# The shared-expert stage of a two-layer transformer block: weights loaded during the last batch, its rows kept in SBUF, the router and the tables of tiles reordered

## The reference

```python
scores = sigmoid(gate_w @ x) + gate_b            # 16 experts
weights, indices = top_k(scores, 4); weights /= weights.sum()
shared_out = (silu(x @ w1_shared) * (x @ w3_shared)) @ w2_shared
h3 = silu((x @ w1_routed[e]) * (x @ w3_routed[e]))
return shared_out + sum_over_chosen_e(weight_e * (h3 @ w2_routed[e]))
```

## Time and profile before

| | |
|---|---|
| time, median of 3 runs | 1366.03 us (1360.82 to 1368.21) |
| the profiled execution | 1364.2 us, its span 1362.4 us |
| busy in the span | PE 1257.5 us (92%), DVE 847.7 us (62%), ACT 596.2 us (44%), POOL 472.7 us (35%) |
| granted PE clock, mean | 0.975 of full speed |
| DMA | 112.20 MB, mean 82 GB/s |

### The profile page before, as it was taken

The page is one execution under the profiler, slowest core; times in us unless marked ns, Lnnn a source line. Parts: engine busy times, 40 slices in busy tenths (PEclk is TensorE's granted clock), DMA queues, the critical chain, the costliest instruction groups (busy, mean ns, idle before and its releaser), DMA issues.

```text
span 1362.4 us, 25374 instructions
## 1 busy us (share of the span) xinstructions
PE 1257.5 (92%) x9326; PEld 1095.7 (80%) x9326; DVE 847.7 (62%) x1733; ACT 596.2 (44%) x1351; POOL 472.7 (35%) x488
## 2 busy tenths in 40 slices
PE   5699989999988879999988899999999999999996
PEld 4588878778777757777767888899999999998995
DVE  4647567557556654434447777776666767676785
ACT  3333323323323335555544444445454545555552
POOL 0112332332431220000028787644434344434442
PEclk9799999989999989999999999999999999999998
DMA  5754224234100953333331221100000000000000
GB/s 203 280 194 152 104 103 151 78 129 148 47 33 27 346 188 105 105 103 103 109 121 53 67 65 47 63 1 32 1 1 32 1 32 1 1 1 1 1 32 32
DMA packets 63674, 112.20 MB, mean 82 GB/s; under 512 B 6977, under 2 KB 36033, under 8 KB 62017
## 3 DMA queue, kind: packets, MB, share of 16 engines
q1 hardware_dynamic: 57408, 93.79, 19.6%
q0 software_dynamic: 6144, 16.79, 3.7%
HBM read 49.86 MB, written 60.69 MB: 81 GB/s over the span
## 4 chain that ended last, share of the span: by engine, by line
PE 82%; DVE 8%; issue 4%; ACT 3%; another core or an unknown queue 2%; DMA 1%; POOL 0%; SPq 0%; ACTq 0%; DVEq 0%; POOLq 0%
PE bank L703 7%; PE six L720 6%; PE six L817 5%; PE bank L779 4%; PE bank L781 4%; PE bank L780 4%; PE bank L390 4%; PE bank L391 3%; PE bank L392 3%; PE bank L854 2%; PE bank L853 2%; PE bank L852 2%; PE bank L791 2%; PE six L831 2%; PE bank L792 2%
## 5 line engine op out<-in xcount | busy, mean ns | idle before, releaser
L1799 POOL TENSOR_TENSOR rstd<-msq,half_pow 128x8 f32<-128x8 f32 x64 | 105.4, 1647 | 156.6 <-DVE msq L1610 156.2
L1128 ACT ACTIVATE pT<-six,rstd 128x256 f32<-128x256 f32 x128 | 60.7, 475 | 215.3 <-PE six L818 212.9
L1736 POOL TENSOR_TENSOR hid_l<-hid,hid_h 128x256 fp32r<-128x256 f32 x64 | 48.0, 750 | 241.2 <-ACT hid_h L950 241.2
L1811 POOL TENSOR_TENSOR pT<-pT,tri_mul 128x512 f32<-128x512 f32 x64 | 84.3, 1316 | 129.1 <-ACT pT L1174 129.1
L1212 DVE TENSOR_TENSOR yT1l<-six,yT1h 128x512 fp32r<-128x512 f32 x64 | 44.3, 692 | 135.5 <-ACT yT1h L1179 135.5
L1603 DVE TENSOR_TENSOR sq<-xs 128x512 f32<-128x512 f32 x128 | 104.2, 814 | 17.2 <-ACT xs L1147 17.2
L703 PE MATMUL bank<-experts,xT 128*128 x316 | 109.5, 469 | 0.8 <-ACT xT L1072 0.8
L779 PE MATMUL bank<-bw_h,xT1h 128*128 128x512 f32 x256 | 106.2, 415 | 0.7 <-issue 0.7
L781 PE MATMUL bank<-bw_l,xT1h 128*128 128x512 f32 x256 | 100.5, 392 | 0.0
L780 PE MATMUL bank<-bw_h,xT1l 128*128 128x512 f32 x256 | 100.1, 391 | 0.0
L817 PE MATMUL six<-qT,kT 128*128 128x256 f32 x256 | 79.3, 392 | 19.0 <-issue 15.6
(11 more groups left out here) (282 smaller groups left out, 3926.7 us busy)
## 6 DMA issues: line engine op xcount, KB each, us to landing
cells_scratch<-zeros SPq DMA_DIRECT2D x8, 4352.0 KB, 14.8
xg<-cells_scratch SPq DMA_DIRECT2D x79, 128.0 KB, 2.0
cells_scratch<-y SPq DMA_DIRECT2D x79, 128.0 KB, 1.7
experts<-pack_experts_dram SPq DMA_DIRECT2D x16, 608.0 KB
raw<-pack_attn_dram SPq DMA_DIRECT2D x8, 1024.0 KB
raw<-pack_w_dram SPq DMA_DIRECT2D x2, 1024.0 KB
xT_scratch<-xT1h_c SPq DMA_DIRECT2D x8, 256.0 KB, 2.1
xT_scratch<-xT1l_c SPq DMA_DIRECT2D x8, 256.0 KB, 2.7
```

Of the source, the lines that this page charges most:

```text
L1799: pool.tensor_tensor(out=rstd[:, r, :], in0=msq[:, r, :], in1=half_pow[:], op=ALU.pow).then_inc(rstd_sb, 1)
```

## The change

- **Loads.** During batch 7 SP already issues the `xT1h` loads of sequences 0 to 5, once the last keys are made (`xT1h` lies where layer 0's query and key weights were), and experts 0 to 5 and `xT1h` of sequence 6 once the last scores are transposed; the `xT1l` loads and experts 6 to 10 follow when the last up projections and the last mix of values are made, and experts 11 to 15 where the loads used to begin. The SBUF layout is reordered so that dead tensors lie under these loads (`w2_h`, `w2_l`, `yt0` and what is used longest move to the end).
- **Sequence 7's transposed norm** is written straight to its place in `xT1h`/`xT1l` (`own_h`, `own_l`, by a `norm_T1_last` on ACT and DVE). Its store and loads and the wait between them are gone.
- **Order at the end of batch 7.** DVE does `out_T` and `gate_out` behind router part 1 of sequence 6 and ahead of parts 2 to 4, which used to come before them; ACT does `out_T` ahead of `gate_out`.
- **Router.** Its steps are split anew. For sequence 7, DVE normalises at m = 2 and makes part 0 at m = 5, each ahead of the tile's own steps, ranks and selection (1, 2) at m = 6, slots (6) at m = 7 and weights (5) at m = 8. PE makes transposes and logits ahead of the tile's `shared_up` at m = 3 and 4 and the positions at m = 7; ACT follows.
- **Tables.** Each partition works out one tile: the steps are 16 columns wide instead of 1280 (`own_tile` is a column 0 to 127 that comes as a constant). Two small matmuls (`tables_T`, m = 12) turn the two columns into a row, the second one packing four experts into a number, and one DVE copy (`tables_row`) hands it on. The steps start at m = 9 instead of 11.
- SP reads the registers of the first eight cells before its wait for the sends instead of behind it.

```diff
@@ -313,27 +320,41 @@
-            def load_norm(b):
-                sp.wait_ge(xT1_stored, 32 * (b + 1) if b == NB - 1 else 32 * (NB - 1))
-                for s, part in enumerate((xT1h, xT1l)):
-                    sp.dma_start(part[:, :, b * T:(b + 1) * T].bitcast(F32),
-                                 xT1_dram[s, b].rearrange("p (k t) -> p k t", k=KD)).then_inc(xT1_loaded[b], 16)
+            def load_norm(b, s):
+                sp.dma_start((xT1h, xT1l)[s][:, :, b * T:(b + 1) * T].bitcast(F32),
+                             xT1_dram[s, b].rearrange("p (k t) -> p k t", k=KD)).then_inc(xT1_loaded[b], 16)
...
-            for b in range(NB - 1):
+            last = NB - 1
+            for b in range(last - 1):
...
+            sp.wait_ge(k0_ps, 2 * NB)
+            sp.wait_ge(xT1_stored, 32 * (last - 1))
+            for b in range(last - 1):
+                load_norm(b, 0)
+            store_norm(last - 1)
+            sp.wait_ge(sT0_ps, NG * NB)
+            sp.wait_ge(cells_cleared, 16 * NB)
+            for e in range(6):
+                load_expert(e)
+            sp.wait_ge(xT1_stored, 32 * last)
+            load_norm(last - 1, 0)
+            sp.wait_ge(y0_ps, NG * NB)
+            sp.wait_ge(up_ps, NJ * NB)
+            for b in range(last):
+                load_norm(b, 1)
+            for e in range(6, 11):
+                load_expert(e)
             sp.wait_ge(yT0_ps, NB)
-            for b in range(NB - 1):
-                load_norm(b)
-            for e in range(10):
-                load_expert(e)
-            store_norm(NB - 1)
-            load_norm(NB - 1)
-            for e in range(10, NE):
+            for e in range(11, NE):
...
@@ -355,8 +376,8 @@
             sp.wait_ge(tables_made, 1)
+            c = cells(0, GROUP)
             sp.wait_ge(cells_sent, 16 * TT * TOPK * NB)
-            c = cells(0, GROUP)
...
@@ -512,6 +533,13 @@
+            def tables_T(bank):
+                pe.wait_ge(tile_cols, 2)
+                n = NG1 * GROUP
+                pe.matmul(bank[0:1, 0:n], t_cols[:, 0:1], ident[:, 0:n], start=True, stop=True)
+                pe.matmul(bank[0:1, n:n + n // PACK], t_cols[:, 1:2], pack_by_4, start=True, stop=True).then_inc(tile_rows, 1)
...
@@ -724,15 +752,17 @@
                     pe.wait_ge(slot_sb, NB)
-                shared_up(m)
...
                 if m == 4:
-                    logits_T(t, six[:, 1, :])
-                if m == 5:
+                    logits_T(t, six[:, 1, :], (own_h, own_l))
+                shared_up(m)
+                if m == 4:
                     logits(t, six[:, 0, :])
-                if m == 9:
+                if m == 7:
                     positions(t, six[:, 1, :], True)
+                if m == 12:
+                    tables_T(six[:, 0, :])
...
@@ -1346,18 +1384,19 @@
                 if part == 2:
+                    link(dve.tensor_tensor(out=r_sel[:], in0=r_rank[:].unsqueeze(2).to_broadcast(kths),
+                                           in1=kth.unsqueeze(1).unsqueeze(3).to_broadcast(kths), op=ALU.is_equal))
+                if part in (3, 5):
...
                                            op=ALU.mult))
-                    link(dve.tensor_tensor(out=r_sel[:], in0=r_rank[:].unsqueeze(2).to_broadcast(kths),
-                                           in1=kth.unsqueeze(1).unsqueeze(3).to_broadcast(kths), op=ALU.is_equal))
...
                     link(dve.tensor_reduce(out=prob_all[:, bass.ds(TT * b, TT), :], in_=r_tmp[:], axis=AX.X, op=ALU.add))
-                if part == 3:
+                if part in (4, 6):
...
@@ -1458,11 +1497,16 @@
                     router(t, 1)
+                if final:
+                    out_T(b)
+                    gate_out(b)
+                if not first:
                     router(t, 2)
+                    router(t, 3)
...
                 if not first:
-                    router(t, 3)
+                    router(t, 4)
...
@@ -1516,23 +1558,19 @@
                 link(dve.tensor_tensor(out=t_end[:], in0=t_first[:], in1=t_count[:], op=ALU.add))
-                link(dve.tensor_tensor(out=t_ge[:], in0=tile_index.unsqueeze(2).to_broadcast(wide),
-                                       in1=t_end[:].unsqueeze(1).to_broadcast(wide), op=ALU.is_ge))
+                link(dve.tensor_tensor(out=t_ge[:], in0=own_tile.to_broadcast([P, NE]), in1=t_end[:], op=ALU.is_ge))
                 link(dve.tensor_reduce(out=t_expert[:], in_=t_ge[:], axis=AX.X, op=ALU.add))
-                link(dve.tensor_tensor(out=t_base[:], in0=t_ge[:], in1=t_count[:].unsqueeze(1).to_broadcast(wide),
-                                       op=ALU.mult))
+                link(dve.tensor_tensor(out=t_base[:], in0=t_ge[:], in1=t_count[:], op=ALU.mult))
                 link(dve.tensor_reduce(out=t_before[:], in_=t_base[:], axis=AX.X, op=ALU.add))
-                link(dve.tensor_tensor(out=t_before[:], in0=tile_index, in1=t_before[:], op=ALU.subtract))
-                link(dve.scalar_tensor_tensor(out=t_before[:], in0=t_expert[:], scalar=float(NT), in1=t_before[:],
-                                              op0=ALU.mult, op1=ALU.add))
-                link(dve.tensor_scalar(out=t_expert[:], in0=t_expert[:], scalar1=float(NE - 1), scalar2=None, op0=ALU.min))
-                dve.tensor_copy(tile_cell[:], t_before[:])
-                four = t_expert[:].rearrange("p (n k) -> p n k", k=PACK)
-                for k in (2, 1):
-                    link(dve.scalar_tensor_tensor(out=four[:, :, k], in0=four[:, :, k + 1], scalar=float(NE),
-                                                  in1=four[:, :, k], op0=ALU.mult, op1=ALU.add))
-                dve.scalar_tensor_tensor(out=tile_pack[:], in0=four[:, :, 1], scalar=float(NE), in1=four[:, :, 0],
-                                         op0=ALU.mult, op1=ALU.add).then_inc(tables_made, 1)
+                link(dve.tensor_tensor(out=t_before[:], in0=own_tile, in1=t_before[:], op=ALU.subtract))
+                dve.scalar_tensor_tensor(out=t_cols[:, 0:1], in0=t_expert[:], scalar=float(NT), in1=t_before[:],
+                                         op0=ALU.mult, op1=ALU.add).then_inc(tile_cols, 1)
+                dve.tensor_scalar(out=t_cols[:, 1:2], in0=t_expert[:], scalar1=float(NE - 1), scalar2=None, op0=ALU.min)\
+                   .then_inc(tile_cols, 1)
+            def tables_row(bank):
+                dve.wait_ge(tile_rows, 1)
+                dve.tensor_copy(tile_row[0:1, :], bank[0:1, 0:NG1 * GROUP + NG1 * GROUP // PACK]).then_inc(tables_made, 1)
...
@@ -1566,26 +1604,29 @@
             for m in range(NS):
+                if m == 2:
+                    normalise(t, xn1_last, mv1, rs1, rs1_sb, xn1_sb)
+                if m == 3:
+                    norm_T1_last(t, six[:, 0, :])
+                if m == 5:
+                    router(t, 0)
...
                     stats(t, st1, mv1, ve1, st1_sb, mv1_sb, ve1_sb, NB)
-                if m == 2:
-                    normalise(t, xn1_last, mv1, rs1, rs1_sb, xn1_sb)
-                if m == 3:
-                    norm_T1(t, six[:, 0, :])
                 if m == 6:
-                    router(t, 0)
+                    router(t, 1)
+                    router(t, 2)
                 if m == 7:
-                    router(t, 1)
+                    router(t, 6, six[:, 1, :], True)
                 if m == 8:
-                    router(t, 2)
+                    router(t, 5)
                 if m == 9:
-                    router(t, 3, six[:, 1, :], True)
-                if m == 11:
                     tables()
+                if m == 12:
+                    tables_row(six[:, 0, :])
...
```

More of the change, by code:

```diff
@@ L148, in build @@
         g1 = sc("g1", [P, NT, D])
+        own_h, own_l = (part[:, :, (NB - 1) * T:NB * T] for part in (xT1h, xT1l))
         sc = region(XT_END, LATE)
@@ L225, in build @@
             "kT1_sb", "rden1_sb", "y1_sb", "yT1l_sb", "acc1", "bw_lo", "v1_ones"))
[L227 to L228 removed]
+        sh_hi, sh_lo, table, tile_cols, tile_rows, tables_made, experts_loaded = (sem(n) for n in (
+            "sh_hi", "sh_lo", "table", "tile_cols", "tile_rows", "tables_made", "experts_loaded"))
         xg_loaded = [sem(f"xg_loaded{j}") for j in range(GROUP)]
@@ L493, in logits_T @@
                 for k in range(KD):
-                    last = three(bank[:, 0:T], gate[0][:, k, :], gate[1][:, k, :], xT1h_c[:, k, :], xT1l_c[:, k, :],
+                    last = three(bank[:, 0:T], gate[0][:, k, :], gate[1][:, k, :], xT1[0][:, k, :], xT1[1][:, k, :],
                                  k == 0, k == KD - 1)
@@ L678, in shared_up @@
                 after(pe, u2_sb, m - 1)
-                if m % TT == 0:
+                if m % TT == 0 and m // TT < NB - 1:
                     pe.wait_ge(xT1_loaded[m // TT], 32)
@@ L961, in norm_T1, with norm_T1_last @@
                 act.activation(xT1h_c[:].rearrange("p k t -> p (k t)"), bank, ACT.Copy).then_inc(xT1h_sb, 1)
+            def norm_T1_last(b, bank):
```

(18 more changed lines are left out.)

33 lines of the change are left out of this document (15 added, 18 removed).

## The result

The kernel with the change takes 1358.9 us (median of 20 runs, 1356.2 to 1363.4). Beside it on the same chip the kernel before took 1364.0 us (20 runs, 1360.4 to 1369.6). The ratio is 0.9963, with a 95% interval of 0.9952 to 0.9974: 5.1 us. That is clear of the noise, but under the 0.5% at which the prediction puts its line. 1359.2 was forecast. The profiled execution took 1357.2 us, 7.0 less than that of before.

What follows compares the result with a forecast made beforehand. PE, busy 92% of the span, was taken as the bound, with 18.1 us excess in the shared-expert stage. Terms 0 + 0.7 - 0.9 - 7.8 + 0.4 + 1.7 = -5.9 us gave 1359.2 us, range 1354 to 1364.5.

Steps and rivals of the forecast that it cites:

- The tables (-7.8): Shared stage: DVE's tables block shrinks from 9.7 to 3.6 us, PE's stall from 9.7 to 1.9; gain 7.8 us.
- The row of tables: Two small PE matmuls and one DVE copy at m = 12 cost 0.4 us, bounds 0.2 and 1.5.
- The sends of sequence 7 (+1.7): Shared stage: 5 to 10 us after sends begin, PE's results reach others late; costs 1.7 us, bounds 0 and 3.9.
- The end of batch 7 (+0.7): Reordered end of batch 7: first up product 0.3 us later, first tiles at half clock 0.4; bounds 0 and 1.7.
- The router (-0.9): Sequence 7's norm and router moved earlier in the shared stage gain 0.9 us; bounds a loss of 1.0, gain of 2.8.
- m = 7 starts about 1.5 us later than before: Part of the router term: the earlier norm and router delay shared tile m = 7 by about 1.5 us.
- With a stall of 1.7 us already paid: Part of the router term: by m = 7 a stall of 1.7 us is already paid, giving net 0.9 us.
- still fall on it: POOL's first sends, starting at 451.04 whatever is changed, still fall on router part 0, now at m = 5.
- Neither the expert weights nor sequence 7's norm set the start: Routed stage's start: PE's last tiles, made late by DVE, set it; SP issues row loads 4.6 us ahead.
- the sends are hidden: Rival, 0.27: sequence 7's sends cost nothing and the logits tile loses its whole excess; -9.5 us, about 1355.5.
- One wait for another: Rival, 0.25: sends' stall, router part 0, half clock and slower first tiles add up; -1.7 us, about 1364.
- The loads hurt batch 7: Rival, 0.06: weight loads from 429 on delay instruction fetches at batch 7's end; +9.7 us, about 1375.

Runs made afterwards that it cites:

- f1: The changed kernel unchanged, on a chip without late answers, beside the kernel before (1336.6 us): 1328.7 us, ratio 0.994.
- e6: The kernel before with the new tables, their row at m = 14, and sequence 7's norm kept in SBUF: 1364.6 us, ratio 0.999.
- e3: The changed kernel without the sends of sequence 7, so its output lacks rows, on a chip without late answers: 1328.6 us (one run).
- e4: The changed kernel without any sends of rows or the waits for them, on a chip without late answers: 1329.5 us, ratio 0.9942 to the kernel before.
- f3: The changed kernel without any sends again, on a chip without late answers: 1330.0 us, ratio 0.9949 to the kernel before.
- second pair: Profiles of the kernel before and the changed kernel, both unchanged, on a chip with late answers: 1368.0 us (one run) and 1362.5 us.
- e1: The kernel before with the new tables alone, at m = 11, their row at m = 14: 1337.3 us, ratio 1.0005.
- r_before: The kernel before, unchanged, run for its profile on a chip with late answers: 1368.0 us (one run).
- r_after: The changed kernel, unchanged, on a chip with late answers: 1362.5 us, ratio 0.9978 to the kernel before.
- f2: The changed kernel with all norm and weight loads issued at the old place, on a chip without late answers: 1329.1 us, ratio 0.9942 to the kernel before.
- e5: The kernel before with sequence 7's norm kept in SBUF alone, no store, wait or reload: 1365.9 us, ratio 1.0004.

## Why the prediction was right in its total, and where it was not

**The tables (-7.8) were right**, with the rest of the change in place. The block is 3.3 us (3.6 forecast). Tile m = 11 takes 4.02 us, 1.97 over the undisturbed 2.05 (1.9 forecast); before, the tables' tile and the next lost 9.24 + 0.46 = 9.7. The clock stayed full. **The row of tables** cost 2.52 - 2.05 = 0.47 us at m = 12 in f1, where nothing else disturbs that tile (+0.4).

**The sends of sequence 7 (+1.7)** came out in size: from m = 11 on the changed kernel takes 15.17 us where answers are late and 13.36 in f1 where they aren't, 1.8 us, most of it in tile m = 12 (4.10 against 2.52), in the expected place, 10 us behind the first send. In e6 the sends start 9.4 us later (479.91), and the wait of DVE for "remote" comes with them: it ends at 489.25, 9.3 us behind the first send, and in the changed kernel at 480.43, 10.0 behind. So the lateness follows the sends in time. But the row of tables moved along with them, to m = 14, and no run takes the sends away where answers are late, so the cause is not shown. Without late answers the sends cost nothing (e3, e4, f3), and both kernels without sends ran where none are late. It stays open whether sends alone bring them on; batch 1, which sends nothing and waits 3.3 us, still speaks for it.

**The end of batch 7 (+0.7)** was +0.35 in this pair. The 0.3 was right. The half clock did come: m = 0 to 2 ran at a mean granted clock of 0.73 of full speed (partly 1.2, partly 2.4 GHz), against 0.82 before, and PE was busy for all 6.27 us instead of 5.65; it cost nothing here because the old order had 0.6 us of waits in these tiles. In the second pair the two rows of the table are +0.86 and -0.06. In e1 and f1, the old and the new order where no answers are late, they are +0.37 and +1.23 (clock 0.96 and 0.75 in m = 0 to 2): up to 1.6 us, near the upper bound.

**The router (-0.9) is the step that failed: the gain isn't there.** m = 3 to 10 take +0.98 us in this pair (24.03 to 25.01) and -0.10 in r_before and r_after (26.51 to 26.41). Only where no answers are late is it -1.0 (21.39 us in e1, with the old order, and 20.35 in f1). The working had two parts. "m = 7 starts about 1.5 us later than before" was +2.3 us from the last `out_T` in this pair, +1.6 in the second and +1.5 between e1 and f1: right but for the first. "With a stall of 1.7 us already paid" was to give that back and more. It gave back 1.0, 0.9 and 1.0, since a stall came in that the prediction has at nothing: `positions`, moved up to m = 7, stands one tile behind the steps that feed it, and PE waits 0.81 us for `r_cum` (0.82 in f1, f2 and f3). Together with the end of batch 7, the way from the last `out_T` to m = 11 was forecast 0.2 us shorter and is 1.3, 0.7 and 0.6 us longer.

What made the first part worse in this pair is the late answers of sequence 6's sends, which "still fall on it". Over e1 and f1 they cost 24.03 - 21.39 = 2.6 us in the old order and 25.01 - 20.35 = 4.7 in the new one. Of the 4.7, m = 4 and 5 have 0.9 and 3.6 (3.10 and 5.63 us against 2.18 and 2.05); m = 6, with router part 0, takes 3.96 against 3.78, so its own stall is paid in full behind the late answer, as it was three tiles later in the old order. In the second pair the same sums are 5.1 and 6.1 us, part of it a half clock in both (0.94 and 0.87 over m = 3 to 10). The sums set traces of different chips against each other, so they price the late answers and don't explain them.

**"Neither the expert weights nor sequence 7's norm set the start" was true of the kernel before, and wrong as a price.** The early loads are worth nothing where no answers are late (f1 against f2, 0.03 us in the stretch). The norm in SBUF is also worth nothing alone (e5), but without it and the earlier router the tables' term is nothing too (e1: 6.62 us of wait for `xg`). I read 4.6 us between SP's issue and PE's transpose as slack of the chain. It was time that the table stall had made: take 9 us off PE, and the chain of store, 15.4 us of landing, reload, six experts, sends that land beside them, and rows is late. The sum was right because the change brings all the parts; its split over them was not.

The sum by its own terms is 0.35 + 0 + 0.98 - 5.43 = -4.1 us against -5.9; it is 4.8 in the second pair of traces, and the median fell by 5.1. The forecast put the level of the kernel before at 1364.2 + 0.9 = 1365.1 us, and beside the change it was 1364.0: 1.1 us too high there, 0.8 too much gain, and so 0.3 us off in all, partly by luck. The rival "the sends are hidden" is what happens without late answers: 8 us, 0.994. "One wait for another" (whose terms add up to 1363.4 us, not 1364) happened in part, at m = 4 to 6. "The loads hurt batch 7" is out: the first weight loads are issued at 425.4, and from the last stored norm to the last `out_T` it is 16.50 us with them (419.56 to 436.06) and 16.46 before (422.88 to 439.34); f1 and f2 have 16.49 and 16.51. The Trainium skill (Runtime: NRT & Kernel Launch, Instruction fetch mechanics) has instruction fetches as mostly hidden, and these 16.5 us agree. Whether fetches have a part in the late answers no run here shows.

## What to carry to other kernels

Time between an issue and its use that lies under a stall is not slack: before pricing the removal of a stall, lay out every chain that ends behind it without the stall, and price the parts of a change together (here 0 and 0 alone; as a pair 3.7 us in the profiled execution, which the timed runs don't confirm; 4.8 with the rest of the change). A wait moved next to another one is only free if both run side by side, not if the second begins with what the first brings. And a step moved earlier may come to stand too close behind the steps that feed it: look for that wait before counting the gain. A long block of linked steps on an engine that feeds PE can be cut in two around the tile's own steps: with two such cuts and `positions` put behind the down products, three gaps of 1.5, 0.8 and 1.7 us became one of 0.6.

## What the hardware showed that was not expected

The same program ran at two levels on different chips, 1364 to 1365 us and 1336.6 us, a 2% gap that is five times this change. PE's undisturbed tile takes 2.05 us on both, and the mean granted clock differs by about 0.01 (0.976 and 0.978 in r_before and r_after, 0.987 in f1_after). Between the changed kernel's profile of the first result and f1_after the spans differ by 28.4 us: 21.3 of them lie ahead of the last `out_T`, 5.9 in the stretch and 1.2 behind it. Ahead of it, DVE's wait for `gate` is 7.2 us against 3.4 in each of batches 2 to 7; six times 3.8 is 23 us. On the faster chips the wait names PE as its releaser, on the others none. The change is worth 8 us (0.994) on the faster chips and 3 to 5 us (0.9963, 0.9978) on the slower ones. Two differences read above add up to about that, as an estimate: 1.8 to 1.9 us from m = 11 on, where sequence 7's late answers no longer lie under the tables, and 0.9 to 2.0 us in m = 3 to 10. What makes the answers late is open.
